# Layer-1 context attention of a two-lane perceiver kernel: scores once, from f16 pairs, with the queries standing on the partitions

## The reference, cut to what matters

```python
# layer 0, one head of 256
attn = softmax((x1 @ Wq + bq) @ (ctx @ Wk + bk).T / 16)
x = x + attn @ (ctx @ Wv + bv)
# layer 1, 16 heads of 16
q = latents @ w_q.T;  k, v = split(ctx @ w_kv.T)
attn = softmax(einsum('blhd,bshd->bhls', q, k) * 16**-0.5)
x = x + einsum('bhls,bshd->blhd', attn, v).reshape(B, L, 256) @ w_out.T + b_out
```

## Time and profile before

| | us |
|---|---|
| runs | 3319.53, 3310.01, 3318.12 (median 3318.12) |
| span of the profiled execution | 3369.6 |
| the same execution's own time around the span | not shown separately |
| TensorE busy in it | 2701.8 (80%) |
| TensorE weight loads | 2102.4 (62%) |
| VectorE | 1869.2 (55%) |
| ScalarE | 1046.4 (31%) |
| GpSimd | 495.2 (15%) |

### The profile page before, as it was taken

The page is one execution under the profiler, slowest core; times in us unless marked ns, Lnnn a source line. Parts: engine busy times, 40 slices in busy tenths (PEclk is TensorE's granted clock), DMA queues, the critical chain, the costliest instruction groups (busy, mean ns, idle before and its releaser), DMA issues.

```text
span 3369.6 us, 114292 instructions
## 1 busy us (share of the span) xinstructions
PE 2701.8 (80%) x45688; PEld 2102.4 (62%) x45783; DVE 1869.2 (55%) x5000; ACT 1046.4 (31%) x2120; POOL 495.2 (15%) x616
## 2 busy tenths in 40 slices
PE   3788888888888888888888887787788888858882
PEld 3566666676676676676676675566666666646662
DVE  4555556655655655655655655555555555545555
ACT  1333333333333333333333333222222222212220
POOL 2111111111111111111111111011111111112221
PEclk9889989988998998998999998899999999979996
DMA  5011111111111111111111112200000000021225
GB/s 176 22 38 50 30 38 51 30 41 48 31 43 44 32 42 44 32 43 44 32 43 43 33 45 72 96 14 17 14 14 14 16 14 14 14 73 62 69 66 178
DMA packets 86140, 153.57 MB, mean 46 GB/s; under 512 B 11224, under 2 KB 39904, under 8 KB 84576
## 3 DMA queue, kind: packets, MB, share of 16 engines
q1 hardware_dynamic: 73136, 117.78, 11.5%
q0 software_dynamic: 6528, 17.87, 1.4%
q10 hardware_dynamic: 6192, 13.38, 1.1%
HBM read 120.37 MB, written 28.62 MB: 44 GB/s over the span
## 4 chain that ended last, share of the span: by engine, by line
issue 54%; PE 24%; DVE 8%; POOL 6%; ACT 3%; DMA 2%; DVEq 2%; SPq 0%; POOLq 0%; ACTq 0%
PE ps L381 15%; POOL mem L463 3%; PE ps L1164 2%; PE ps L1479 2%; POOL x L1036 2%; PE ps L1116 1%; POOL rstd L1030 1%; DVEq L1457 1%; DVE mem L1348 1%; DVE mem L1527 1%; DMA y_tok<-mem 1%; DVE mem L1322 1%; DVE mem L1378 1%; DVE mem L1379 1%; DVE mem L1382 1%
## 5 line engine op out<-in xcount | busy, mean ns | idle before, releaser
L381 PE MATMUL ps<-mem 128*128 128x256 f16 (+1 forms) x4224 | 566.2, 293 | 76.1 <-DVE mem L1348 66.9
L381 PEld LDWEIGHTS ps<-mem 128*128 128x128 f16 x4224 | 439.2, 106 | 168.4 <-DVE mem L1348 70.4
L788 ACT ACTIVATE mem<-ps 128x512 f32<-128x512 f32 (+3 forms) x320 | 177.5, 565 | 430.6 <-PE ps L742 135.1
L381 PE MATMUL ps<-xt,mem 128*128 128x128 f16 x4608 | 280.4, 220 | 30.0 <-DVE xt L1303 30.0
L381 PEld LDWEIGHTS ps<-xt,mem 128*128 128x128 f16 x4608 | 261.4, 98 | 40.4 <-DVE xt L1303 37.4
L1030 POOL TENSOR_TENSOR rstd<-var_eps,neg_half 128x1 f32<-128x1 f32 x128 | 70.4, 550 | 1210.8 <-DVE var_eps L889 1210.8
L463 POOL TENSOR_TENSOR mem<-mem 128x514 f16<-128x514 f32 x136 | 161.1, 1187 | 569.2 <-ACT mem L458 569.2
L1004 DVE COPY mem<-ps 128x514 f32<-128x514 f32 x128 | 88.9, 694 | 262.8 <-PE ps L381 262.8
L1014 DVE RECIPROCAL mem<-ps 128x64 f32<-128x64 f32 x256 | 142.6, 557 | 161.9 <-PE ps L735 160.3
L832 ACT ACTIVATE mem<-ps 128x512 f32<-128x512 f32 x256 | 152.3, 595 | 174.9 <-PE ps L715 174.5
L715 PE MATMUL ps<-mem 64*128 64x128 f32 x2048 | 201.1, 319 | 0.0
(11 more groups left out here) (256 smaller groups left out, 5056.9 us busy)
## 6 DMA issues: line engine op xcount, KB each, us to landing
mem<-in_ctx_t SPq DMA_DIRECT2D x136, 257.0 KB, 2.8
mem<-in_ctx_n SPq DMA_DIRECT2D x136, 256.0 KB, 3.3
mem<-x_sorted SPq DMA_DIRECT2D x74, 128.5 KB
mem<-y_pairs SPq DMA_DIRECT2D x32, 256.0 KB, 4.1
mem<-in_experts ACTq DMA_DIRECT2D x7, 768.0 KB, 9.1
x<-in_x_tok SPq DMA_DIRECT2D x34, 128.0 KB, 3.5
x_mid<-x SPq DMA_DIRECT2D x32, 128.0 KB, 1.8
x<-x_mid SPq DMA_DIRECT2D x32, 128.0 KB, 2.0
```

What stands on the lines that cost most here:

```text
L381: last = pe.matmul(dst, a, b, start=i == 0 and j == 0, stop=i == n - 1 and j == 2)
L788: act.activation(dst, src, ACT.Copy).then_inc(*did(done))
```

## The change

Layer 0: the context product now has the probabilities as weights (32 columns a sequence, one column group each) and the context rows moving, 256 columns; the result has rows on the partitions, is copied (`a1_f`), turned by two transposes (`at1_ps`) and copied again.

Layer 1: queries, masks and keys are kept as f16 pairs (`q4`, `qbd`, `kp`, high by ScalarE from PSUM, low by a subtraction on VectorE). Scores are made once, of three products of pairs, queries on the partitions. ScalarE takes the exponentials with the maximum as bias and sums the row in the same instruction, two instructions a unit. Probabilities are turned by TensorE, copied by ScalarE, and multiplied by the values into one bank that gathers all units. No product with ones. The last key's probabilities of all units are turned by one product (`last_turned`) and multiplied in `last_values`. The sums' reciprocals (16 columns) are spread by four products (`spread_sums`), and one multiplication follows the selection of heads. `keys_to_values(0)` and `(1)` come ahead of the hidden row's transposes and wait for `r3`; key blocks use other banks. All orders of the first loop and of the joint to the second are new. Buffers have new places.

The diff, cut (new lines; what they replace is in the listing above):

```diff
-        tensor=("oyoyoyyooooyooyoyooooyoyooyooooyoooyoyooyooooooyyooyyooyoo"),
+        tensor=("oooooyoyoyoyoooyooyoyoyooyoyyooyoooooyooyoooyoooooooooyoyyyoy"),
-        scalar=("oyyyoooyoyooooooyooyoooyyoyooyoyyoooooyoyyooo"),
+        scalar=("oooyooyyoooyoyoooyoyoooyoooyyoooyoooyoyyooooooyyy"),
-        vector=("yyyyoyoooooyyoyyyoyyooooyyoyyyoyoooyooooyooyyyyyooyyooyyyyoyoyyyooyyyyooyyooyyooyooyoyyyyyo"),
+        vector=("yoyyyyoooooyyooyyyoooooyoooooyoyyyyyoyooyyooyyoyyoyooyyoyyyyyyyyyyyyyoooyyyyyyyyyyo"),
-        gpsimd=("yoyyoooyoyo"),
-        sync=("yyyyyyyyooo"),
+        gpsimd=("yyoooyooyyo"),
+        sync=("yyyyoyyoyyo"),
...
+                for m in range(2):
+                    for b in range(NB):
+                        pe.matmul(ps[SEQ * b:SEQ * (b + 1), 2, 0:D], pt1[:, m * P + SEQ * b:m * P + SEQ * (b + 1)], ctx_nf[:, b, m, :], start=(m == 0), stop=False)
+                pe.matmul(ps[:, 2, 0:D], pt1[:, 256:384], ctx_lf, start=False, stop=True).then_inc(*did("a1_ps"))
+                yield
+                need("a1_f")
                 for c in range(C):
...
+                    last = pe.transpose(ps[:, 1, c * P:(c + 1) * P], a1[:, c * P:(c + 1) * P], ident)
+                last.then_inc(*did("at1_ps"))
+                yield
+                need("at1_f")
...
                 def keys_to_values(b):
-                    if b >= 2:
+                    if b < 2:
+                        need("r3", b + 1)
+                    else:
                         need("v4_f", b - 1)
...
                 def scores(u):
                     b, c = u // 2, u % 2
...
+                    need("k4_l", max(b + 1, 3 + c) if u < 2 else b + 1)
+                    if u >= 2:
+                        need("exp4", 2 * (u - 2) + 2)
+                    for j, (a, r) in enumerate(((0, 0), (0, 1), (1, 0))):
+                        for i in range(2):
+                            rows = slice(64 * i, 64 * i + 64)
+                            last = pe.matmul(ps[:, 2 * c + i, 0:KEYS], qbd[rows, a, c, b].rearrange("p h q -> p (h q)"), kp[rows, r, c, b, :],
+                                             start=(j == 0), stop=(j == 2))
+                    last.then_inc(*did("s4_ps"))
+                    yield
+
+                def turned(v):
+
+                    if v < 2:
+                        need("exp4", 2 * (UNITS - 2) + 2)
                     else:
...
+                        need("pt4_f", v - 1)
                     for i in range(2):
...
+                        for m in range(2):
+                            last = pe.transpose(ps[:, v % 2, (2 * i + m) * P:(2 * i + m + 1) * P], prob4[:, v, i, m * P:(m + 1) * P], ident)
+                    last.then_inc(*did("t4_ps"))
+                    yield
+
+                def values(v):
+                    b, c = v // 2, v % 2
+                    need("pt4_f", v + 1)
+                    for m in range(2):
+                        for r in range(4):
+                            i, part = r // 2, slice(64 * (r % 2), 64 * (r % 2) + 64)
+                            last = pe.matmul(ps[SEQ * r:SEQ * (r + 1), 3, 64 * (NB * c + b):64 * (NB * c + b) + 64], vp[:, b, m, P * c + SEQ * r:P * c + SEQ * (r + 1)],
+                                             pt4[:, v % 2, i, m, part], start=(v == 0 and m == 0), stop=(v == UNITS - 1 and m == 1))
+                    last.then_inc(*did("o4_ps"))
+                    yield
...
+                def last_turned():
...
+                    need("last_a")
+                    pe.matmul(ps[:, 2, 0:P], last_a, sel.unsqueeze(1).to_broadcast([P, NB, SEQ]), start=True, stop=True).then_inc(*did("pl_ps"))
...
+                def last_values():
...
+                    need("pl_m")
+                    for c in range(C):
+                        last = pe.matmul(ps[:, 2, c * P:(c + 1) * P], vl_m[:, c * P:(c + 1) * P], pl_m, start=True, stop=True)
...
+                def spread_sums():
...
+                    need("last_f")
+                    need("rb_b")
                     for c in range(C):
                         for i in range(2):
...
+                            last = pe.matmul(ps[64 * i:64 * i + 64, 2, c * P:(c + 1) * P], heads, rb_b[:, 2 * c + i].rearrange("p b q -> p (b q)"), start=True, stop=True)
...
+                def key_hi(b):
+                    bank = KEY_BANKS[b]
+                    yield from act_copy(act, t, kp[:, 0, :, b], ps[:, bank:bank + 2, 0:KEYS], "k4_h", "k4_ps", b + 1)
+
+                def exponentials(u):
+                    c = u % 2
+                    act.wait_ge(*at(t, "s4_max", u + 1))
+                    for i in range(2):
+                        act.activation(prob4[:, u, i], ps[:, 2 * c + i, 0:KEYS], ACT.Exp, bias=neg_max[:, u, i:i + 1],
+                                       accum_out=sums[:, 0, 2 * u + i:2 * u + i + 1]).then_inc(*did("exp4"))
+                    yield
+
+                def turned_out(v):
+                    if v >= 2:
+                        act.wait_ge(*at(t, "o4_ps", v - 1))
+                    yield from act_copy(act, t, pt4[:, v % 2].rearrange("p i m n -> p (i m n)"), ps[:, v % 2, :], "pt4_f", "t4_ps", v + 1)
```

## The result

| | before | forecast | after |
|---|---|---|---|
| median of the runs, us | 3318.41 | 3028 | 2988.11 |
| ratio, 95% interval | | 0.913 | 0.900 (0.8985 to 0.9016) |
| period of the first loop, us | 62.97 | 53.7 | 52.67 |
| granted clock in it | 0.91 | | 0.97 |

A forecast was written before the change was run, and what follows sets the result against it. TensorE bounds the first loop, but not alone: 40.4 us work and about 10 idle make 50.6, plus 3.1 for clock, 53.7 against 62.97 a period. Saving 290 from 3318 gives 3028 us; range 2940 to 3225.

The forecast's parts named there:

- work at 2.4 GHz: TensorE, first loop, per tile: probabilities -8.2, scores +2.6, last key -0.5, layer-0 context product -2.3; sum -8.4 us.
- clock: First loop: time lost per period to TensorE's lower clock, taken as 5 us before and 3.1 after (bounds 0 and 7).
- idle: First loop: TensorE idle 9.2 us a period before, about 10 after, new waits replacing old ones of the same total.
- the walk: Durations added along the four engines' orders in one first-loop period, 0.1 us per handing over, full clock: 50.6 us.
- the price of loads in series: Scores on TensorE: alternative estimate with six weight loads in series, 0.64 us a unit instead of 0.50.
- two falls: First loop: low clock in two places again, around the 14 to 29 us stretch and the tile boundary; 3.1 us added.
- Gate: End of part 1: gate transposes wait for a layer norm on VectorE until 39.5 us; 1.5 us of TensorE idle.
- I scale the saving by 0.985: Profiled span 3369.6 us is 1.6% above the median 3318.12, so the 295 us saving was reduced to 290.
- neither fall: Low clock from scores(0) to y4, 3421 us, chance 0.09; or only from turned(0) to y4, 3239 us, chance 0.05.
- units of scores overlap: Rival: scores go one at a time, 2.65 us a unit, period 60, 3220 us; chance 0.05.
- column groups of 256 columns run side by side: Rival: in the layer-0 context product they do not overlap, 3 us more, period 56.7, 3122 us; chance 0.07.
- Less idle, clock stays: Rival: first-loop period 50.6 us, 2932 us in all; chance 0.10.

The follow-up runs named there:

- the kernel's second profile: The kernel before the change, unedited, profiled again: span 3324.1 us, time 3325.99 us.
- the pairs run: Changed kernel with turned and values of two units grouped (values, values, turned, turned): 3055.94 us, ratio 0.9191.
- the value blocks behind the hidden row: Changed kernel with the values of context blocks 0 and 1 behind the hidden row's transposes again, as before: 3183.35 us, ratio 0.9578.
- two scores earlier: Changed kernel with scores(5) between the other tile's qk and v, scores(7) ahead of its self-attention scores, matching steps earlier: 3057.6 us, ratio 0.9195.

## Why the prediction came out as it did

The sign, the range and the main mechanism, less work on TensorE with the idle time left much as it was, were right; the saving was under-estimated by 40 us of 330. That it came so near is in part luck: the saving of work was over-estimated by 2 to 3 us a period, and what the clock and the idle time would give back was under-estimated by more, 3.4 to 3.9 together. Per period, with the kernel's second profile beside the one that I used (its records are fuller, 28806 products against 28706):

| term | forecast | by the first profile | by the second |
|---|---|---|---|
| work at 2.4 GHz | -8.4 | 48.8 to 43.2: -5.6 | 49.4 to 43.2: -6.2 |
| clock | 5 to 3.1: -1.9 | 5 to 1.3: -3.7 | -3.7 |
| idle | 9.2 to 10.2: +1.0 | 9.2 to 8.1: -1.1 | 8.7 to 8.1: -0.6 |
| period | -9.3 | -10.3 | -10.5 |

Forecast idle is the walk's 50.6 less 40.4 of work; the gaps that it lists sum to 9.8. The 5 us of before stay an estimate from the earlier trace rows, and the split between work and clock with it; after's 1.3 is measured.

**Work.** Over-estimated by 2 to 3 us, the term that missed by most. The unit of turned and values costs 0.89, not 0.75: transposes 0.53 where two in a row gave 0.21, rounds 0.36 where one gave 0.13. Eight units, 1.1 us. I took 0.06 for the change of shape, once; the pairs run shows about 0.2 for two units that change half as often. The last-key steps sum to 1.55, not 1.2; the layer-0 product to 2.0, not 1.7 (the full product 0.63, not 0.5; its transposes 0.37, not 0.21). Scores came near the forecast, 0.55 for 0.50; the price of loads in series, 0.64, is refuted by pairs 0.11 us apart. By these prices the parts sum to 8 x (0.89 - 1.77) = -7.0 for the probabilities, 8 x (0.55 - 0.17) = +3.0 for the scores, -0.2 for the last key and -2.0 for layer 0: -6.2, the second profile's difference. Only the last of them was also taken back by itself; the others rest on the timelines.

**Clock.** Off by 1.8 us, to the good side. I forecast two falls; there is one. The value blocks ahead of the hidden row keep TensorE at work where the earlier trace rows show it at 0.10 of 2 us; without them 3.5 us of busy time come back. I counted those blocks as cover for VectorE's tail only.

**Idle.** 8.1 for 10.2, the places half right. Last key: 1.4, and 0.4 ahead of turned(0), 1.8 forecast. Gate: 0.9 and 0.3, 1.5 forecast. Hidden row: 1.3 and 0.7, 1.6 forecast. Scores: 0.3 where 4 were forecast. An exponential with its accumulator read follows the last at 0.45 us, not 0.57, some 1.9 us in sixteen, which is most of why ScalarE is at 28.5 and not 31; how much of the scores' waits it saved was not tried. The probabilities of layer 0 cost no wait. Not foreseen: 2.2 us at the second layer norm, of which GpSimd's subtraction makes 0.8. The walk held GpSimd's steps to be waited for by nobody; one of them slows its neighbour on VectorE.

**The scale.** "I scale the saving by 0.985" was wrong: the long span was one execution's stops in the second loop. Unscaled the forecast is 3023 us.

**The rivals.** The clock rose from 0.91 to 0.97, so neither fall came; units of scores overlap (0.3 us of waits a period); column groups of 256 columns run side by side (four in 0.50 us). "Less idle, clock stays" is what came in part, and more work than forecast hid it.

## What to carry to other kernels

When TensorE is the bound and its clock isn't at 1.00 all through, price each gap twice: by its length and by what runs at the lower level behind it; in three edits here (the value blocks behind the hidden row, pairs, two scores earlier) the same products took more busy time at a lower clock than the waits grew by. Look at what GpSimd does beside each VectorE instruction that is on the path, from SBUF to SBUF above all. And where one span is a per cent above its median, look for the place before scaling anything.

## Unexpected on the chip

A normalisation of 128x256 f32 on VectorE took 410 ns, and 1210 beside a GpSimd subtraction. A gap of the same 2.3 us at the same product was followed by 3.4 us at 1.2 GHz in one order and by 6.8 in another, with nothing changed but the order of eight steps. 18 more products a tile in one loop cost 72 us in another, unchanged one, where stops came along with code loads. Products of 257 columns on the two row halves follow one another at 0.11 us a pair, and a unit of them costs 0.1 to 0.2 us on top, once.
